# A decoder layer on one core: the last batch taken out of the loop, and the choice of tokens for the experts split between batches 0 to 2 and batch 3

## The chip, the cores and the metric

One core of a Trainium2 chip runs the whole layer in one launch. The metric is the device time in microseconds (us) of that core; less is better. The median of three runs of the kernel before is 4139.88 us (4139.71 to 4147.63).

## The reference, cut to what matters

Four batches of S = 1024 tokens with D = 512 numbers each pass through self-attention (16 heads, relative bias), a layer norm, causal cross-attention against a context, a second layer norm (its result is called x2 below), a mixture of 16 experts, and a last layer norm. The change is about the experts and what stands just before them.

```python
logits = jnp.einsum('bsd,de->bse', x, Wg) + bg
probs = jax.nn.softmax(logits, axis=-2)          # over the 1024 tokens of a batch
pv = jnp.transpose(probs, (0, 2, 1))             # batch, expert, token
vals, idx = jax.lax.top_k(pv, K)                 # K = 128 tokens per batch and expert
tok = x[bidx, idx]
h = relu(tok @ w1[e] + b1[e]); h = relu(h @ w2[e] + b2[e]); h = h @ w3[e] + b3[e]
outputs = zeros.at[bidx, idx].add(h * vals[..., None])
# then layernorm(x + outputs)
```

Each expert picks its 128 tokens out of every batch by itself, so what batches 0 to 2 send to the experts is known as soon as these batches' x2 is. Batch 3 has no part in it.

## The kernel before, in words

There are two blocks of instructions, one after the other, in which each of the five engines (PE, DVE, ACT, POOL, SP) has its own program. Semaphores tie the programs together. The first block ends at line 1377.

**The first block, attention.** Every engine has a loop over the 4 batches. In one batch: eight pairs of heads of self-attention (`attend`; on DVE `add_biases` for a pair's row tiles 2 to 7 and `cross_border` for tiles 0 and 1 of the next pair, where PE weighs the values in three parts, L1088); the output projection with wo (PE L1173, DVE adds at L837); the first norm; the projections for cross-attention; 48 units of cross-attention (`xscore` L1294, `xturn` L1308, `xweigh` L1323, `turn_back` L1331); the second norm (`normalize_rows`, DVE L714 to L726; ACT takes the root at L536). Then x2 is stored twice by SP (L467), as `x2_d` to gather from and as `y_d` to add to, and its rows are turned (PE L988; the even tiles are copied by ACT L541, the odd ones by DVE L734) and multiplied with Wg to logits (PE L1373), which DVE copies (L972) and SP stores (L475). At its end each iteration already opens self-attention of the next batch: PE projects q and k (L1020, partly in the last units of cross-attention), DVE and ACT copy them (L742, L553) and add the bias and take exponentials of four tiles (L756, L530), POOL scales them (L487), DVE turns them (L781). Batch 3 does this too, for a batch of zeros that nobody reads.

**The second block, choosing.** SP loads all logits as 128 rows (64 of batch and expert, each cut into two halves of 512 tokens; L1481). DVE takes the maximum (L1672), ACT the exponentials (L1588), DVE scales. Then DVE picks the 128 largest of each row in 16 rounds of eight (L1682 to L1685, each instruction followed by a wait for its own end), adds the row's base (L1688), PE turns the two lists (L1804) and reverses the upper halves (L1808), and DVE merges the two halves (L1696 to L1701). POOL gathers the tokens of expert 0 (L1547), PE turns them (L1815), ACT and DVE copy them.

**The second block, experts.** A loop over experts 0 to 13 on every engine. PE runs three layers over all four batches at once, each layer 16 products in two passes (L1830, L1845, L1856; 512 columns). DVE applies bias and relu (L1724), and bias and weight of the result (L1735). POOL gathers the next expert's tokens and adds the results to `y_d` (L1569). DVE turns the gathered tokens in blocks of 32 (L1712), and ACT issues 16 DMAs that spread the blocks into `tokT` (L1599). SP loads the three weights of the next expert, each when PE frees its buffer (L1492). Behind the loop experts 14 and 15 run in six steps, for batches (0, 1), (2) and (3) in turn (`STEPS`; PE L1880, L1892, L1901), with the last norm and the output between them. Their weights are loaded at L1496 and L1500, expert 15's tokens are gathered behind the loop, and SP spreads them with 16 DMAs (L1505) into `last_tokT`.

The order on each engine is written out by hand: an engine that waits holds everything behind it in its program, its DMAs too.

```python
            next_tokens(E - 1)                                # POOL, behind the loop
            ...
            sp.wait_ge(tok_turned, B)                         # SP, L1502
            for g in range(GROUPS):
                for m in range(GROUPS):
                    sp.dma_start(last_tokT[...], tok_blocks[...]).then_inc(last_tokT_loaded, 16)
```

## Time and profile before

| what | value |
|---|---|
| median of three runs | 4139.88 us |
| the profiled execution | 4138.08 us |
| its span, first to last instruction | 4136.3 us |
| mean granted TensorE clock | 0.978 |
| PE busy | 3837.9 us (93%) |
| DVE busy | 2483.1 us (60%) |
| ACT busy | 1566.9 us (38%) |
| POOL busy | 904.0 us (22%) |

Times in the rows are microseconds from the first instruction of the profiled execution, so its own 4138.08 us hold 1.8 us outside the span. The four batches fill the time up to about 3361 us, the choice of tokens the time up to 3434 us, the loop over 14 experts that up to 4011 us, and the steps of the last two experts with the last norm the rest.

### The profile page before, as it was taken

Reading aid. Unit: us, or ns where it says so; the run is one execution under the profiler, and the core shown is the slowest. Engines: PE = TensorE matmul, PEld = TensorE weight load, DVE = VectorE, ACT = ScalarE, POOL = GpSimd, SP = SyncE. Lnnn points to the kernel's source line nnn. Section 1 sums busy time; section 2 is a strip of 40 time slices with the busy share of each in tenths; the row PEclk is TensorE's granted clock in tenths of the full one; section 3 lists DMA queues with packets and bytes.
Section 4 is the critical chain, followed back from the end, with each engine's and each line's share of the span. In section 5 each row is a group of like instructions: output and inputs, shape, how many; then the busy total and the mean of one; then the engine's idle time right before and its main releaser. Section 6 shows DMA issues by size and latency. Waiting matters only on the chain. (4 is left out here: it accounts for less than half of the span.)

```text
span 4136.3 us, 91192 instructions
## 1 busy us (share of the span) xinstructions
PE 3837.9 (93%) x36924; PEld 2346.8 (57%) x36924; DVE 2483.1 (60%) x4839; ACT 1566.9 (38%) x3178; POOL 904.0 (22%) x1017
## 2 busy tenths in 40 slices
PE   5999999999999999999999999999999948999996
PEld 2677645656776456567754565677545623444445
DVE  3777535877775368777744587777446872222224
ACT  2444225854442258544422584444135720000002
POOL 2333200223331012233310022333101202222221
PEclk8999999999999999999999999999999979999998
DMA  8333449744333487443335873433358725666676
GB/s 259 105 92 97 126 169 316 269 130 112 96 95 116 188 310 266 127 116 95 95 104 203 305 265 119 116 96 96 103 221 297 265 86 127 157 147 157 148 181 189
DMA packets 323147, 678.60 MB, mean 164 GB/s; under 512 B 28432, under 2 KB 125760, under 8 KB 319504
## 3 DMA queue, kind: packets, MB, share of 16 engines
q1 hardware_dynamic: 275152, 621.65, 46.9%
q0 software_dynamic: 15024, 34.41, 4.5%
q10 hardware_dynamic: 32576, 16.92, 1.9%
q8 instruction: 291, 4.77, 0.5%
q14 instruction: 104, 0.85, 0.1%
HBM read 388.31 MB, written 210.11 MB: 145 GB/s over the span
## 5 line engine op out<-in xcount | busy, mean ns | idle before, releaser
L530 ACT ACTIVATE sc<-sc,nmax 128x1024 f32<-128x1024 f32 x516 | 591.7, 1147 | 777.0 <-DVE nmax L756 776.4
L487 POOL TENSOR_SCALAR sc<-sc,pinv 128x1024 f32<-128x1024 f32 x516 | 576.5, 1118 | 1198.8 <-DVE pinv L764 1185.6
L1088 PE MATMUL psum<-pts,wct 32*64 32x256 f32 x8192 | 460.2, 376 | 9.0 <-PEq L1083 4.6
L1088 PE MATMUL psum<-xall,wct 32*64 32x256 f32 x8192 | 458.9, 376 | 6.1 <-issue 6.0
L1073 PE MATMUL psum<-xt,w_all 128*128 128x256 f32 x1792 | 415.7, 385 | 23.6 <-PEq L1070 23.6
L886 DVE CUSTOM_DVE_ANT_0 sc<-psum,big 128x896 f32<-128x896 f32 (+7 forms) x512 | 364.0, 753 | 102.9 <-PE psum L1294 87.2
L781 DVE STREAM_TRANSPOSE pts<-sc 128x1024 f32<-128x1024 f32 (+3 forms) x342 | 333.6, 976 | 130.6 <-PE psum L1088 87.0
L1073 PEld LDWEIGHTS psum<-xt,w_all 128*128 128x128 f32 x1792 | 332.5, 190 | 128.3 <-issue 67.0
L530 ACT ACTIVATE sc<-sc,xmax 128x896 f32<-128x896 f32 (+7 forms) x512 | 394.8, 773 | 11.7 <-DVE xmax L886 11.6
L756 DVE CUSTOM_DVE_ANT_0 sc<-psum,table_a 128x1024 f32<-128x1024 f32 x258 | 312.1, 1210 | 110.0 <-PE psum L1031 92.5
L1088 PEld LDWEIGHTS psum<-pts,wct 32*64 32x64 f32 x8192 | 310.6, 132 | 99.8 <-issue 54.8
L502 POOL TENSOR_SCALAR_AFFINE_SELECT big<-big 128x256 f32<-128x256 f32 (+1 forms) x192 | 92.6, 482 | 1146.7 <-DMA big<-skew_d 1146.6
L1088 PEld LDWEIGHTS psum<-xall,wct 32*64 32x64 f32 x8192 | 321.3, 131 | 15.0 <-issue 10.6
L781 DVE STREAM_TRANSPOSE xall<-sc 128x1024 f32<-128x1024 f32 (+3 forms) x342 | 326.9, 956 | 2.7 <-DVEq L710 1.2
L1308 PE MATMUL psum<-ident,sc 128*128 128x128 f32 x2304 | 313.5, 281 | 7.1 <-ACT sc L530 6.1
L756 DVE CUSTOM_DVE_ANT_0 sc<-psum,table_b 128x1024 f32<-128x1024 f32 x258 | 314.6, 1219 | 0.5
L1308 PEld LDWEIGHTS psum<-ident,sc 128*128 128x128 f32 x2304 | 258.6, 142 | 77.8 <-DVE pts L896 39.8
L1031 PE MATMUL psum<-xall 64*128 64x512 f32 x1040 | 264.3, 627 | 26.0 <-ACTq L529 10.4
L1060 PEld LDWEIGHTS psum<-w_all,xt 128*128 128x128 f32 x2048 | 236.5, 192 | 76.5 <-issue 76.5
L1031 PE MATMUL psum<-big,xall 64*128 64x512 f32 x1024 | 254.4, 615 | 10.3 <-ACTq L529 8.1
L1617 ACT ACTIVATE hid<-psum,bias 128x128 f32<-128x128 f32 x32 | 11.7, 367 | 647.7 <-PE psum L1880 638.8
L1060 PE MATMUL psum<-w_all,xt 128*128 128x128 f32 x2048 | 254.7, 280 | 0.8 <-PEq L1058 0.6
(194 smaller groups left out, 5362.0 us busy)
## 6 DMA issues: line engine op xcount, KB each, us to landing
wct<-xall SPq DMA_DIRECT2D x576, 128.0 KB, 2.4
big<-skew_d SPq DMA_DIRECT2D x48, 1024.0 KB, 5.4
w_sb<-w_dram SPq DMA_DIRECT2D x45, 1024.0 KB, 5.7
big<-skew_d SPq DMA_DIRECT2D x48, 768.0 KB, 4.4
big<-skew_d SPq DMA_DIRECT2D x32, 896.0 KB, 5.3
big<-skew_d SPq DMA_DIRECT2D x32, 640.0 KB, 7.0
w_all<-wqkv_dram SPq DMA_DIRECT2D x33, 512.0 KB, 3.5
skew_d<-pts SPq DMA_DIRECT2D x8, 2048.0 KB, 6.6
```

Source lines behind the costliest of these rows:

```text
L487: pool.tensor_scalar(sc[k % 4][:, :], sc[k % 4][:, :], pinv[:, k % 4:k % 4 + 1], 1.0, ALU.mult, ALU.mult).then_inc(probs_scaled, 1)
L502: pool.affine_select(out=near, in_=near, compare_op=ALU.is_ge, fill=-BIG, base=0, pattern=[[0, len(heads)], [-1, P]], channel_multiplier=1 ...
L530: act.activation(tile, tile, ACT.Exp, bias=least, scale=-1.0, accum_out=total).then_inc(probs_ready, 1)
L756: dve.tensor_tensor_reduce(sc[k % 4][:, :], SLOT[h], table[h][:, off:off + S], -1.0, BIG, ALU.add, ALU.min, nmax[:, k % 4:k % 4 + 1]).then ...
L781: ins = dve.transpose(probs_t(h, t, first, last), tile[:, first:last, :])
L886: dve.tensor_tensor_reduce(scx[u % 2][:, at], SCORES[:, at], skw[u % 4][:, at], -XSCALE, BIG, ALU.add, ALU.min, xmax[:, k:k + 1]).then_inc ...
L1031: mm = pe.matmul(psum[:, 2 * h + n, :], qf[which][HEAD[h], P * t:P * t + P], kf[which][HEAD[h], HALF * n:HALF * n + HALF], start=True, sto ...
L1060: mm = pe.matmul(SPARE[m // 2][:, P * (m % 2):P * (m % 2) + P], xt[:, c, P * m:P * m + P], w_sb[:, 2, c, :], start=(c == 0), stop=(c == DC ...
L1073: mm = pe.matmul(SPARE[m], w_sb[:, a, c, :], xt[:, c, QG * m:QG * m + QG], start=(c == 0), stop=(c == DC - 1))
L1088: mm = pe.matmul(OSUM[HEAD[h], a, :], v_all[rows, ST * (b % GROUPS) + b // GROUPS, HEAD[h]], ptf[h][rows, QG * b:QG * b + QG], start=(b == ...
L1308: mm = pe.transpose(TURN[m % 3][:, P * (i % 4):P * (i % 4) + P], scx[u % 2][:, at:at + P], ident[:, :])
L1617: act.activation(hid[layer][:, c, cols], BANK[DC * (1 - layer) + c][:, 0:n], ACT.Relu, bias=(bias1, bias2)[layer][:, e:e + 1]).then_inc(st ...
```

## The change

The loops over batches run over batches 0 to 2, and batch 3 is written out behind them (`batch(B - 1, last=True)`).

In batch 3: SP loads the logits of batches 0 to 2 (96 rows) into the upper half of `xr`; DVE runs their selection among the pairs of self-attention, twelve rounds of eight picks at the borders of pairs and four when the output projection begins; PE turns and reverses the lists at row tiles 5 and 6 of the output projection; POOL gathers expert 0's tokens of these batches in the middle of cross-attention, and SP loads w1 and w2 of expert 0 there instead of what the batch of zeros needed. The opening of a fifth batch is gone. The logits of batch 3 are not stored; SP moves them inside SBUF with 8 DMAs.

In the second block: experts 0 to 2 run in three steps over batches 0 to 2 (384 columns), with weights of their own for experts 1 and 2, and then in three steps over batch 3 alone (128 columns). ACT applies bias, relu and weights in these six steps. DVE meanwhile selects for batch 3 (32 rows), and a round of eight picks waits for itself twice instead of three times. PE turns the lists in the step of expert 2. Expert 15's tokens are gathered and spread, and its weights loaded, before the loop. The loop covers experts 3 to 13, and the six steps of experts 14 and 15 stand behind it as before.

```diff
+FIRST_EXPERTS = (0, 1, 2)
+F = len(FIRST_EXPERTS)
+SOONER, LATER = (0, 1, 2), (3,)
-STEPS = [(e, group) for group in FINISH for e in LAST_EXPERTS]
+STEPS = [(e, group) for group in (SOONER, LATER) for e in FIRST_EXPERTS] + \
+        [(e, group) for group in FINISH for e in LAST_EXPERTS]
+BEHIND = 2 * F
...
+            def pick(r):
+                now = held[r][0:n, :]
+                eight = top[0:n, 8 * r:8 * r + 8]
+                done(dve.max(eight, now))
+                ins = dve.max_index(top_at[0:n, 8 * r:8 * r + 8], eight, now)
+                if r < PICKS - 1:
+                    ins = dve.match_replace(held[r + 1][0:n, :], eight, now, -1.0)
+                done(ins)
...
# DVE, batch 3
+                    row_max()
+                    cross_border(scale_rows)
+                    add_biases()
+                    pick(0)
+                    for hp in range(2, PAIRS):
+                        cross_border(lambda: pick(2 * hp - 3))
+                        add_biases()
+                        if hp < PAIRS - 1:
+                            pick(2 * hp - 2)
+                    dve.wait_ge(y_ready, 1)
+                    for r in range(2 * PAIRS - 4, PICKS):
+                        pick(r)
+                    number_rows()
...
# SP, batch 3: the second half of xr once the picks are made; at its end the logits
+                    sp.wait_ge(picked, 1)
+                    sp.dma_start(xr[:, ST // 2:ST, :], x[b, HALF:S, :]...).then_inc(xr_loaded, 16)
...
+                    for i in range(2):
+                        for j in range(2):
+                            for k in range(2):
+                                g = 2 * (i ^ j) + k
+                                sp.dma_start(last_pr[E * i:E * i + E, j, QG * k:QG * k + QG],
+                                             last_lg[DH * g:DH * g + E, :]).then_inc(lg_loaded, 16)
...
# PE, batch 3
+                if last:
+                    first_tokens(pe, 0)
+                    transpose_rows()
...
# POOL, batch 3, middle of cross-attention
+                    if last and u == NU // 2:
+                        pool.wait_ge(picks_done, 1)
+                        pool.wait_ge(xt_free, 1)
+                        for b in SOONER:
+                            pool.indirect_dma_start(tok[:, b, :], None, x2_d[0:S * len(SOONER), :], ...)
...
# SP, second block, ahead of the loop (w3 of expert 0, weights of experts 1 and 2, then expert 15's)
+            sp.wait_ge(early_turned, B)
+            sp.sem_inc(tok_free, 1)
+            sp.wait_ge(tokT_free, 1)
+            sp.sem_inc(tokT_free, -1)
+            spread(tokT, tok_blocks, tokT_loaded)
+            sp.wait_ge(early_turned, 2 * B)
+            sp.sem_inc(tok_free, 1)
+            spread(last_tokT, last_blocks, last_tokT_loaded)
-            with sp.Fori(0, E - 2) as e:
+            with sp.Fori(F, E - 2) as e:
                 for n, w in enumerate((w1, w2, w3)):
                     sp.wait_ge(we_free[n], 1)
...
# POOL, second block
+            gather_sooner(1)
+            for s in range(F):
+                for i in range(2):
+                    scatter(s, i)
+                if s + 2 < F:
+                    gather_sooner(s + 2)
+                scatter(s, 2)
+                if s + 2 == F:
+                    gather_later()                 # waits for picks_done of batch 3
+            pool.wait_ge(first_turned, DC * (F + 1))
+            gather(F)
+            gather_last()                          # waits for tok_free
+            for s in range(F, BEHIND):
+                scatter(s, 0)
...
# ACT, second block
+            for s in range(F):
+                bend(s, 0)
+                bend(s, 1)
+                if s == 0:
+                    row_exps(act, 1, last_pr[0:2 * LATER_ROWS, :, :])
+                    act.wait_ge(bias3_scaled, 1)
+                take_y(s, 0)
+                take_y(s, 1)
+                copy_first_tokens(act, s + 1, tokT if s < F - 1 else later_tokT)
+                take_y(s, 2)
...
# PE, second block, in take_step(s): first layer
+                    mm.then_inc(step_hid_full, 1)
+                    if s == F - 1 and o == 0:
+                        turn_picks(pe, 1, row_no[:, :], (BANK[0][:, 0:P], BANK[0][:, P:2 * P]))
+                    if s == F - 1 and o == 1:
+                        flip_picks(pe, 1, LATER_ROWS, flip[:, :], lists, BANK[1][:, 0:2 * LATER_ROWS])
...
+            for s in range(BEHIND):
+                take_step(s)
+            pe.wait_ge(step_y_taken, TAKEN[BEHIND])
             pe.sem_inc(y_taken, B)
-            with pe.Fori(0, E - 2) as e:
+            with pe.Fori(F, E - 2):
```

New names used below: `first_tokens` turns the gathered tokens of three batches on PE (12 transposes), `bend` is bias and relu on ACT, `take_y` bias and weight on ACT, `spread` the 16 DMAs from turned blocks to the layout that PE reads.

## Rows read from the trace of the kernel before

**Rows 1.** The page, busy tenths of 40 equal slices (103.4 us each).

```profile
PE   5999999999999999999999999999999948999996
PEclk8999999999999999999999999999999979999998
```

**Rows 2.** Windows: stretch, length, busy us (x instructions) by engine, clock, DMA share, GB/s.

```profile
3390.00:3400.00 10.00, 0.00 (x0) 0.00 (x0) 8.39 (x19) 0.00 (x0) 0.00 (x0) 0.50 0.00 1
```

**Rows 3.** Timeline, end of batch 3: start us, us, engine, line, what.

```profile
3340.43 3.74 DVE L726 TENSOR_SCALAR xr<-xr,mv,rstd 128x512 f32<-128x512 f32 x8 [0.15 <-DVEq L710]
...
3357.20 0.69 DVE L734 COPY wct<-psum 128x512 f32<-128x512 f32 x1
...
3358.75 1.92 PE L1373 MATMUL psum<-wct,wg_sb 128*16 128x256 f32 x32 [1.83 <-PEq L995]
...
3361.80 1.86 SPq L475 DMA_DIRECT2D logit_d<-big  x4
...
3364.03 1.20 DVE L781 STREAM_TRANSPOSE xall<-sc 128x1024 f32<-128x1024 f32 x1
3365.49 2.46 SPq L1481 DMA_DIRECT2D pr<-logit_d  x4
```

**Rows 4.** Timeline, choosing tokens.

```profile
3370.25 1.22 DVE L1672 TENSOR_REDUCE rmax<-pr 128x1 f32<-128x1024 f32 x1 [5.03 <-DMA pr<-logit_d]
...
3374.62 0.69 DVE L1682 MAX8 top<-pr 128x8 f32<-128x512 f32 x1
...
3377.27 0.70 DVE L1682 MAX8 top<-left 128x8 f32<-128x512 f32 x1
...
3416.51 0.48 PE L1804 MATMUL psum<-ident,row_no 128*128 128x128 f32 x1 [55.84 <-DVE row_no L1688]
...
3429.49 3.30 PE L1815 MATMUL psum<-ident,tok 128*128 128x128 f32 x16 [10.86 <-DMA tok<-x_d,idx_g]
...
3433.90 13.97 PE L1830 MATMUL psum<-tokT,w_sb 128*128 128x512 f32 x32 [1.10 <-PEq L1828]
```

**Rows 5.** Groups by line and form, 3434 to 4010 us.

```profile
L1830 PE MATMUL psum<-tokT,w_sb 128*128 128x512 f32 x448 | 194.6, 592 | 1.1 <-PEq L1828 1.1
```

**Rows 6.** Timeline, from the end of the loop on.

```profile
4010.77 7.07 PE L1880 MATMUL psum<-tokT,w_sb 128*128 128x256 f32 x32
...
4023.13 0.95 POOL L1547 DMA_INDIRECT tok<-x_d,idx_g  x1 [0.30 <-issue]
...
4027.69 10.56 SPq L1505 DMA_DIRECT2D last_tokT<-tok_blocks  x16
...
4040.64 10.14 PE L1880 MATMUL psum<-last_tokT,last_w 128*128 128x256 f32 x32 [7.13 <-DMA last_tokT<-tok_blocks]
...
4064.39 3.73 PE L1880 MATMUL psum<-tokT,w_sb 128*128 128x128 f32 x32
...
4075.02 3.73 PE L1880 MATMUL psum<-last_tokT,last_w 128*128 128x128 f32 x32
```

**Rows 7.** Timeline of DVE at a border of two pairs of heads, batch 3.

```profile
2733.60 1.25 DVE L781 STREAM_TRANSPOSE xall<-sc 128x1024 f32<-128x1024 f32 x1
2735.46 1.23 DVE L756 CUSTOM_DVE_ANT_0 sc<-psum,table_a 128x1024 f32<-128x1024 f32 x1 [0.62 <-PE psum L1031]
...
2742.71 0.71 DVE L781 STREAM_TRANSPOSE pts<-sc 128x512 f32<-128x512 f32 x1 [3.30 <-PE psum L1088]
...
2751.83 0.45 DVE L781 STREAM_TRANSPOSE pts<-sc 128x256 f32<-128x256 f32 x1 [1.00 <-ACTq L581]
```

**Rows 8.** Timeline of DVE in the output projection, batch 3.

```profile
2961.88 0.69 DVE L837 TENSOR_TENSOR xr<-psum,xr 128x512 f32<-128x512 f32 x1 [20.01 <-PE psum L1173]
...
2983.34 0.69 DVE L837 TENSOR_TENSOR xr<-psum,xr 128x512 f32<-128x512 f32 x1 [5.24 <-PE psum L1173]
```

**Rows 9.** DMA issues in 3440 to 3900 us: what, count, KB each, median us to landing.

```profile
w_sb<-w_dram SPq DMA_DIRECT2D x34, 1024.0 KB, 5.7
...
tok<-x_d,idx_g POOLq DMA_INDIRECT x44, 3.7
```

595 lines of the change are left out of this document (382 added, 213 removed).

## The prediction, made before the changed kernel ran

> **What bounds the kernel now.** I read the slices of the page first. PE is the engine that is busy nearly always, at full clock, and there is one dip besides the end [rows 1]. A window in that dip shows PE idle and the clock at 0.50, while DVE alone works [rows 2]. So elsewhere the time is PE's work, and here it is a chain. The timeline gives the chain in two pieces. First, the end of batch 3: DVE normalises x2 until 3344.2, PE turns the rows in between other work until DVE's last copy ends at 3357.9, the logits are multiplied from 3358.75 to 3360.7, SP stores them at 3361.8, and SP's next load comes at 3365.49, right behind DVE's last turn for the batch of zeros, which ends at 3365.2 [rows 3]: the blocks are closed by all engines together. Second, the choice: it starts at 3370.25, a round of eight picks takes 3377.27 - 3374.62 = 2.65 us and there are 16, the lists are turned at 3416.5, the first tokens reach PE at 3429.5, and the first expert's product starts at 3433.9 [rows 4]. From the logits' end (3360.7) to there PE does some 4 us of work in 73 us.
>
> The experts themselves are PE from end to end: 448 products of the first layer have 1.1 us of idle before them in all [rows 5]. Fourteen passes of the loop take 4010.77 - 3433.90 = 576.9 us, 41.2 us each [rows 4, 6].
>
> The last thing to see stands behind the loop. Expert 14's step on batches 0 and 1 starts at 4010.77, expert 15's at 4040.64, after a wait of 7.13 us for `last_tokT`, and expert 15's ends at 4064.39 [rows 6]. At 256 columns a layer of 16 products takes half of 41.2 / 3, and the third layer of two batches the same, so a step is 20.6 us. The first took 29.9 and the second 23.75 (its first layer ran 10.14 us where the step before needed 7.07: PE had stood still and restarted slowly). Together 12.4 us are lost there to the late gather and its 16 DMAs.
>
> **The change part by part.** I follow the time at which the loop over the remaining experts can start, against 3433.9 + 3 x 41.2 = 3557.5, when the kernel before has done experts 0 to 2.
>
> *End of batch 3.* With no fifth batch, PE turns the rows at once. DVE's odd copies start at 3343.9 (0.4 us is won, because PE's q products no longer stand in front of the last turns of cross-attention), and there are four of them (0.69 us each), with PE's four transposes and two handoffs between; I take 1.8 us for each period, so 3350.2. Logits 1.92, DVE's copy and the handoffs 0.9: 3353.2. Then SP issues 8 small DMAs before it can close its block. Four took 1.86 us at L475 and four 2.46 at L1481 [rows 3], mean 0.54, so 8 cost 4.3. With handoffs and slower transposes (PE is idle for some 5 us before them) the second block starts at 3359; from 3356 to 3362.
>
> *Three steps over batches 0 to 2.* 384 columns are three quarters of 41.2 us: 30.9 each, 92.7 us. PE has stood 5 us, so it starts at half the clock, as expert 15's step did, which lost 3.07 us [rows 6]; I take 3.0. Turning the next tokens: 16 transposes took 3.30 us at the low clock [rows 4], so 12 at the full one take 1.3; with the switch 1.5, three times: 4.5. Turning and reversing batch 3's lists in the third step: 1.5 (PE 0.5 + 0.7 and handoffs). The weights hide: a load lands in 5.7 us [rows 9], and before the second step 4 are wanted, 22.8 us even one after the other, against more than 30.
>
> Does batch 3's selection come in time? ACT's exponentials stand behind two layers' `bend`, so they start about 3.0 + 20.6 + 0.7 us into the block. Exponentials with their table 3, DVE's scaling 1.2, 16 rounds at 2.65 less 0.2 for the wait dropped = 39.2, row numbers 0.4: picks at 68.1 us into the block. PE wants them after 3.0 + 61.8 + 3.0 + 2.6 = 70.4. A margin of 2 us, so nothing is waited for; if a round takes 2.65 still, 1 us is.
>
> So the three steps end at 3359 + 3.0 + 92.7 + 4.5 + 1.5 = 3460.7.
>
> *Three steps over batch 3.* A step of one batch took 4075.02 - 4064.39 = 10.63 us [rows 6], although a quarter of 41.2 is 10.3. Three: 31.9, so PE is ready for the loop at 3492.6. But is the loop? Its first w1 is issued by SP behind two `spread`s, and those wait for gathers. POOL adds the last result of the third step (2.7 us with ACT's part), then copies indices and gathers 4 tiles for expert 3: the last gather is issued some 5 us later, 8.3 us behind the step's end. From a last gather's issue to SP's first spread DMA it took 4027.69 - 4023.13 = 4.6 us, and 16 such DMAs hold SP's queue for 10.56 us [rows 6]. Expert 15's gathers start only when the blocks are turned; they land and are turned just as the first spread ends (3.8 for the issues, 3.7 to landing [rows 9], 2.5 for DVE = 10.0). Then the second spread, 10.56, then the w1 load, 5.7 [rows 9]. Sum: 8.3 + 4.6 + 10.6 + 10.6 + 5.7 = 39.8 us behind the three steps, against PE's 31.9. **PE waits some 8 us for w1**, as long as the wait in rows 6, so I charge the slow restart again, 3.0. The loop is as good as started at 3460.7 + 39.8 + 3.0 = 3503.5. That is 54.0 us sooner than 3557.5.
>
> The Trainium skill has a rule against this step, in "DMA: Bandwidth & Descriptors", section "Issuing engines are not separate DMA queues": issuing from several engines saves only sequencer time, usually small beside the transfer. By it the 32 DMAs in front of w1 would cost little; the row has 10.56 us of SP's queue for 1 MB, and I go by the row.
>
> *Behind the loop.* Gather, turn, spread and weights of expert 15 are gone from there: 12.4 us are won, and the rest of the tail follows PE.
>
> *Costs in batch 3.* Twelve rounds of 2.45 us on DVE in self-attention. At a border, DVE idles 0.6 us before `open_pair(0)` and 3.3 us before the turn that waits for PE [rows 7]; the round placed there fits. The other round, between pairs, pushes the opening by 1.9 us, and the two together push the turns by about 1.1; the next idle microsecond (before 2751.83) takes it up. Nearest rows say 0; bounds 0 and 12 x 2.45 = 29.4. I take 1.0. Four more rounds when the projection begins: 10 us from 2961.9, while PE begins its fifth tile one period (5.24 + 0.69 + 0.93) before 2983.34, at 2976.5, and needs only the first sum for it; DVE idles 5.2 us before each later tile [rows 8], so nothing but PE's three list instructions: 1.5. POOL's three gathers in cross-attention hold its queue for 4 us; they cost 0 if its masks are made that far ahead, and 4 if they are wanted at once. POOL is busy for 22% of the time, so I take 0.
>
> **The sum:** 54.0 + 12.4 - 1.0 - 1.5 = 63.9. The profiled execution had 4138.08, 1.8 less than the median 4139.88, so 4074.2 against it and **4076.0** as a median.
>
> **The rivals.** (a) *The forecast*: w1 late behind the spreads. 4076, from 4068 to 4084 by the bounds of the block's start (3 each way), of the restarts (0 to 6) and of the pairs. Chance 0.55.
>
> (b) *w1 is not waited for*: the issue queue moves faster than in rows 6, because nothing else loads then, or PE's small steps take longer than 10.6 with their handoffs to ACT. PE is the bound throughout; 10.9 us more are won: 4065, to 4061 with an early start of the block. This is what the skill's rule above would give. For it: the buffer of w1 is free some 25 us before the load is issued. Against: 16 DMAs held ACT's and SP's queues alike. Chance 0.2.
>
> (c) *The selection costs on both sides*: the rounds are on the path in half of the borders (15 us), or the picks of batch 3 come a few us after PE wants them (my margin is 2). 4084 to 4100, typically 4090. For it: 0.6 us is all the idle time before a pair's opening. Chance 0.2.
>
> (d) *Slower*: PE runs dry at the borders, and each time its clock falls. The place is the border of two pairs, 12 rounds. The gain without them is 64.9 us; a round costs what it delays, 2.45, if both waits of rows 7 move with it 4.9, and with a restart at half clock 3.07 more: 8.0, 96 us in all, so 4171. It decides from (64.9 + 8.3) / 12 = 6.1 us a round. [...] Chance 0.03.
>
> (e) *The change doesn't do what it says*: PE's steps wait for batch 3's picks anyway, through one of the queues (POOL waits for `picks_done` with adds behind it, ACT for the exponentials). Then only the phantom batch's end, some 6 us, and the 12.4 remain: about 4122. Against it: in no queue does a step of batches 0 to 2 stand behind such a wait before the third. Chance 0.02.
>
> **How the numbers follow.** The forecast is (a)'s, 4076. The range takes (a), (b) and most of (c): 4061 to 4096. The measurement tells some 0.2% from no change, 8.3 us. Faster 0.95 ((a), (b), (c) nearly whole, (e)); slower 0.03, from (d); the same 0.02.
>
> **What would show it.** In the profile after: the first product of the experts at about 3359, at clock 0.5; three layers of 16 products of 384 columns, 10.3 us each; the lists turned in the third step with a PE idle below 1 us before it; a wait of PE for w1 ahead of the loop, 8 us, with SP's `last_tokT` spread ending just before the load; no wait for `last_tokT` behind the loop, so 41.2 us for the two steps there; pairs of self-attention in batch 3 as long as in batch 2. Wrong would be: a w1 wait of none (b), or of far more; longer pairs; a wait of PE for the picks.

## The result and the profile after

| | before | changed |
|---|---|---|
| time, median of the runs shown together | 4143.76 us (4139.71 to 4147.98) | 4077.09 us (4071.49 to 4081.91) |
| ratio | | 0.9839, 95% interval 0.9820 to 0.9857 |
| profiled execution: its time, span | 4138.08, 4136.3 us | 4071.49, 4069.7 us |
| TensorE's mean granted clock | 0.978 | 0.984 |

The changed kernel is 1.6% faster. The forecast was 4076.0 us. Between the two profiled executions lie 66.6 us, where the sum said 63.9.

The page of the changed kernel, busy tenths of 40 slices (101.7 us each):

```profile
PE   5999999989999999899999999999999989999997
...
PEclk8999999999999999999999999999999999999998
```

The dip to 4 of [rows 1] is an 8 now, and the clock's 7 beside it is a 9. Two short pauses are what is left of it. Both stand in the timeline of PE, of SP and of DVE at the end of batch 3 and after it (start us, us, engine, line, what, idle time ahead):

```profile
3333.33 0.33 PE L1573 MATMUL psum<-ident,wct 128*128 128x128 f32 x1 [0.38 <-ACT wct L862]
...
3350.58 3.26 PE L1620 MATMUL psum<-wct,wg_sb 128*16 128x256 f32 x32 [1.63 <-issue]
3353.88 0.48 DVE L1193 TENSOR_SCALAR w_and_tables<-psum,bg_sb 128x256 f32<-128x256 f32 x1 [4.20 <-PE psum L1620]
3354.61 5.20 SPq L642 DMA_DIRECT2D w_and_tables<-w_and_tables  x8
3360.65 12.54 PE L2112 MATMUL psum<-xt,w_and_tables 128*128 128x384 f32 x32 [6.82 <-PEq L2088]
...
3394.96 10.48 PE L2112 MATMUL psum<-xt,fin 128*128 128x384 f32 x32
...
3425.94 0.27 DVE L370 TENSOR_SCALAR row_no<-top_at,base_sb 32x128 f32<-32x128 uint32 x1
3427.21 2.74 PE L2112 MATMUL psum<-xt,fin 128*128 128x384 f32 x8
3429.79 0.27 PE L325 MATMUL psum<-ident,row_no 128*128 128x128 f32 x1
...
3459.91 3.73 PE L2112 MATMUL psum<-later_tokT,w_and_tables 128*128 128x128 f32 x32
```

`L2112` is the first layer of a step. The first step starts at 3360.65, right behind SP's 8 DMAs (to 3359.81), and its first layer takes 12.54 us where the second step's takes 10.48: the clock was low. The picks are numbered by 3426.2 (`L370`), and the lists are turned at 3429.79 with no wait, 3.6 us later. The three steps over batches 0 to 2 end at 3459.91. The windows show the clock (stretch, length, busy us by engine, clock, DMA share, GB/s):

```profile
3359.00:3363.00 4.00, 2.35 (x4) 1.47 (x5) 1.70 (x4) 0.00 (x0) 1.56 (x2) 0.50 0.37 80
3363.00:3365.00 2.00, 2.00 (x5) 0.96 (x5) 0.00 (x0) 0.00 (x0) 1.29 (x2) 0.59 1.00 363
3365.00:3395.00 30.00, 30.00 (x95) 16.66 (x94) 6.47 (x18) 10.51 (x19) 4.54 (x4) 1.00 1.03 359
...
3492.00:3498.00 6.00, 0.47 (x2) 0.00 (x0) 0.00 (x0) 0.78 (x1) 1.56 (x1) 0.98 0.68 117
3498.00:3504.00 6.00, 2.28 (x3) 1.17 (x4) 0.00 (x0) 0.00 (x0) 3.12 (x5) 0.50 1.05 390
```

The second pause is the one that the prediction charged, ahead of the loop (SP, ACT, DVE and PE in one timeline):

```profile
3469.09 2.03 DVE L1991 STREAM_TRANSPOSE tok_blocks<-xt 128x512 f32<-128x512 f32 x3 [34.38 <-DMA xt<-x_d,idx_g]
...
3472.22 10.70 SPq L1728 DMA_DIRECT2D xt<-tok_blocks  x16
...
3481.29 2.49 DVE L1991 STREAM_TRANSPOSE last_blocks<-xt 128x512 f32<-128x512 f32 x4 [9.23 <-DMA xt<-x_d,rows]
3483.42 0.78 ACT L1902 ACTIVATE oute<-psum,scaled_bias,vals 128x512 f32<-128x512 f32 x1 [5.12 <-DMA y_d<-oute,rows]
3483.87 10.82 SPq L1728 DMA_DIRECT2D last_tokT<-last_blocks  x16
...
3492.51 0.78 ACT L1902 ACTIVATE oute<-psum,scaled_bias,vals 128x512 f32<-128x512 f32 x1 [3.07 <-PE psum L2146]
...
3495.10 1.00 SPq L1743 DMA_DIRECT2D w_and_tables<-w_dram  x2
...
3501.72 15.40 PE L2170 MATMUL psum<-xt,w_and_tables 128*128 128x512 f32 x32 [9.24 <-PEq L2168]
```

PE had its last result at 3492.5. SP's two spreads stand in front of w1, which goes out at 3495.10, and PE starts the loop at 3501.72, after 9.24 us. Its first 32 products take 15.40 us, where the same 32 in the loop of before took 13.97 [rows 4]. Behind the loop nothing is waited for:

```profile
3956.42 7.07 PE L2112 MATMUL psum<-xt,w_and_tables 128*128 128x256 f32 x32
...
3977.10 7.07 PE L2112 MATMUL psum<-last_tokT,last_w 128*128 128x256 f32 x32
...
3997.78 3.73 PE L2112 MATMUL psum<-xt,w_and_tables 128*128 128x128 f32 x32
```

The two steps take 3997.78 - 3956.42 = 41.36 us; they took 4064.39 - 4010.77 = 53.62 [rows 6].

In batch 3's self-attention, the border that [rows 7] show has become (timeline of DVE):

```profile
2733.66 1.25 DVE L977 STREAM_TRANSPOSE xall<-sc 128x1024 f32<-128x1024 f32 x1
2734.83 0.65 DVE L362 MAX8 top<-xr 96x8 f32<-96x512 f32 x1
...
2737.33 1.23 DVE L952 CUSTOM_DVE_ANT_0 sc<-psum,w_and_tables 128x1024 f32<-128x1024 f32 x1 [0.30 <-DVEq L945]
...
2741.19 0.67 DVE L362 MAX8 top<-xr 96x8 f32<-96x512 f32 x1
```

The opening of the pair comes at 2737.33 instead of 2735.46. One pair earlier the first round starts at 2682.96, so that a pair is 2734.83 - 2682.96 = 51.87 us long, as before the change (51.86 us between the same rows of two pairs): the late opening is made up within the pair. In the output projection four rounds stand ahead of DVE's sums, and PE's later tiles are reached some 0.7 us late (2984.08 for the sum of 2983.34 in [rows 8]), 1.1 us at its end. In these two profiles cross-attention gave even that back: the last turn of batch 3 stands at 3333.33, and it stood at 3333.42. That is one profile of each kernel. From the end of self-attention (DVE's last turn there starts at 2940.50) to that last turn this profile of the changed kernel has 392.8 us, as the one of before has, and all ten profiles of the runs below have 395.4 to 401.5, though none of them edits anything in this stretch. So what the change costs in batch 3 is known to within some 9 us only.

### The profile page after: what moved, and what is told of

Its sections match the earlier page's. It is cut to its first block and busy times, and to the rows that moved or that the text cites. A ratio compares the mean times of both kernels' runs of the same rounds, so it can differ in the third digit from the quotient of the medians.

```text
span 4069.7 us, 91371 instructions
## 1 busy us (share of the span) xinstructions
PE 3828.7 (94%) x37104; PEld 2365.1 (58%) x37104; DVE 2471.1 (61%) x4870; ACT 1598.8 (39%) x3247; POOL 897.9 (22%) x1005
## 5 line engine op out<-in xcount | busy, mean ns | idle before, releaser
L952 DVE CUSTOM_DVE_ANT_0 sc<-psum,w_and_tables 128x1024 f32<-128x1024 f32 x512 | 603.6, 1213 | 97.9 <-PE psum L1267 81.7
L1310 PE MATMUL psum<-xt,w_and_tables 128*128 128x256 f32 x1792 | 415.7, 385 | 23.0 <-PEq L1307 23.0
L1310 PEld LDWEIGHTS psum<-xt,w_and_tables 128*128 128x128 f32 x1792 | 332.5, 190 | 127.7 <-issue 66.3
L1325 PEld LDWEIGHTS psum<-xall,wct 32*64 32x64 f32 x8192 | 324.4, 131 | 17.1 <-issue 12.3
L1550 PEld LDWEIGHTS psum<-ident,sc 128*128 128x128 f32 x2304 | 257.2, 142 | 77.3 <-DVE pts L1122 39.8
L1297 PEld LDWEIGHTS psum<-w_and_tables,xt 128*128 128x128 f32 x2048 | 236.3, 192 | 75.4 <-issue 75.4
L1892 ACT ACTIVATE hid<-psum,bias 128x128 f32<-128x128 f32 (+1 forms) x80 | 34.3, 431 | 594.1 <-PE psum L2112 554.7
L1297 PE MATMUL psum<-w_and_tables,xt 128*128 128x128 f32 x2048 | 254.5, 280 | 0.6 <-PEq L1295 0.5
L1536 PE MATMUL psum<-xall 32*128 32x512 f32 (+3 forms) x1024 | 204.1, 589 | 46.7 <-DVE xmax L1112 34.2
```

Of the source, the lines that this page charges most:

```text
L952: dve.tensor_tensor_reduce(sc[k % 4][:, :], SLOT[h], table[h][:, off:off + S], -1.0, BIG, ALU.add, ALU.min, nmax[:, k % 4:k % 4 + 1]).then ...
L1297: mm = pe.matmul(SPARE[m // 2][:, P * (m % 2):P * (m % 2) + P], xt[:, c, P * m:P * m + P], w_sb[:, 2, c, :], start=(c == 0), stop=(c == DC ...
L1310: mm = pe.matmul(SPARE[m], w_sb[:, a, c, :], xt[:, c, QG * m:QG * m + QG], start=(c == 0), stop=(c == DC - 1))
L1325: mm = pe.matmul(OSUM[HEAD[h], a, :], v_all[rows, ST * (b % GROUPS) + b // GROUPS, HEAD[h]], ptf[h][rows, QG * b:QG * b + QG], start=(b == ...
L1536: mm = pe.matmul(SCORES[:, at:at + m], q, k, start=True, stop=True)
L1550: mm = pe.transpose(TURN[m % 3][:, P * (i % 4):P * (i % 4) + P], scx[u % 2][:, at:at + P], ident[:, :])
```

## The experiments

All are edits of the changed kernel. Their medians carry an interval of about 0.15% (6 us), as wide as most of the effects, and one source of that is visible: the last turn of batch 3, which no edit below touches except the two on the picks, lay between 3333.3 and 3343.4 us in the profiles. So I read stretches of PE's timeline: **border**, from that last turn to the first step; **steps**, from there to the first step over batch 3; **to loop**, from there to the loop's first product; **behind**, the two steps behind the loop.

| run | median us | ratio [95%] | border | steps | to loop | behind |
|---|---|---|---|---|---|---|
| changed kernel | 4077.09 | 0.9839 [0.9820, 0.9857] | 27.32 | 99.26 | 41.81 | 41.36 |
| weights first | 4070.46 | 0.9836 [0.9823, 0.9850] | 28.03 | 99.70 | 38.97 | 41.36 |
| spread behind | 4065.68 | 0.9821 [0.9806, 0.9836] | 28.18 | 99.22 | 35.24 | 41.36 |
| open sooner | 4067.00 | 0.9824 [0.9809, 0.9839] | 23.29 | 97.27 | 42.40 | 41.35 |
| double picks | 4098.46 | 0.9901 [0.9886, 0.9917] | 28.91 | 98.85 | 42.72 | 41.36 |
| three rounds | 4086.28 | 0.9865 [0.9849, 0.9882] | 28.09 | 99.70 | 43.30 | 41.36 |
| late picks | 4082.23 | 0.9856 [0.9841, 0.9871] | 28.05 | 107.93 | 43.21 | 41.36 |
| late picks, early exponentials | 4081.62 | 0.9850 [0.9835, 0.9865] | 27.87 | 99.54 | 42.77 | 41.36 |
| expert 15 late again | 4079.97 | 0.9853 [0.9838, 0.9868] | 28.20 | 99.18 | 33.57 | 53.47 |
| picks first | 4123.98 | 0.9958 [0.9941, 0.9975] | 71.53 | 99.65 | 41.65 | 41.36 |
| together | 4059.11 | 0.9799 [0.9786, 0.9812] | 23.19 | 97.28 | 32.01 | 41.36 |

A stretch is read from one profile of each run, and it varies where nothing was edited. Seven kernels have the same code from the first step over batch 3 to the loop (changed kernel, open sooner, double picks, three rounds, late picks, its companion, picks first): they need 41.65 to 43.30 us for it, and their first 32 products of the loop take 15.40 to 16.76 us. Both together the changed kernel's profile is the lowest, by up to 2.7 us, so a gain at this place that is read against it may be up to 2.7 us too small.

**The overlap itself: picks first.** My theory of the gain was that three steps run where PE stood idle.

```diff
+            row_exps(act, 1, last_pr[0:2 * LATER_ROWS, :, :])
             for s in range(F):
                 bend(s, 0)
                 bend(s, 1)
                 if s == 0:
-                    row_exps(act, 1, last_pr[0:2 * LATER_ROWS, :, :])
                     act.wait_ge(bias3_scaled, 1)
...
+            pe.wait_ge(picked, 2)
             for s in range(BEHIND):
                 take_step(s)
```

> Edit of the changed kernel: TensorE waits for batch 3's picks before the first expert step, and ACT does batch 3's exponentials ahead of the first bends, so that nothing is overlapped with the selection. Theory (the gain of the change is that three steps over batches 0 to 2 run in the time in which PE waited for the picks): the picks come 39.2 us behind the exponentials (3386.99 to 3426.2), these now at about 3365.4, so PE starts the first step at about 3404.6 instead of 3360.65, 44 us later, and 0 to 2 us more for the clock; all that follows keeps its length (steps 97 to 99 us, then 41.8 us to the loop, the two steps behind the loop 41.4 us). Time 4077 + 45 = about 4122, ratio to before 0.994 to 0.997. Rival: the gain is mostly elsewhere (batch 3 written out without a fourth batch's loads, the tail), and this costs under 25 us.

The border is 71.53 us, 44.2 more, and nothing else moved. The row of PE's timeline:

```profile
3414.90 12.93 PE L2112 MATMUL psum<-xt,w_and_tables 128*128 128x384 f32 x32 [49.46 <-PEq L2088]
```

So 44 of the 66.6 us hang on the overlap. By the medians 16 us are left against the kernel before, with an interval of some 7 us either way. By the profiles 12.3 are left behind the loop, and from batch 3's last turn to the end of the loop 9.5 (667.8 us against 677.4), in which the end of batch 3, the cheaper rounds and the tokens gathered ahead of the block are not told apart.

**The wait for w1: weights first, spread behind.**

```diff
+            for n, w in enumerate((w1, w2)):
+                sp.wait_ge(we_free[n], 1)
+                sp.sem_inc(we_free[n], -1)
+                sp.dma_start(w_e[n], w[F].rearrange("(c p) n -> p c n", p=P)).then_inc(we_loaded[n], 16)
             sp.wait_ge(early_turned, B)
             sp.sem_inc(tok_free, 1)
...
+            sp.wait_ge(we_free[2], 1)
+            sp.sem_inc(we_free[2], -1)
+            sp.dma_start(w_e[2], w3[F].rearrange("(c p) n -> p c n", p=P)).then_inc(we_loaded[2], 16)
-            with sp.Fori(F, E - 2) as e:
+            with sp.Fori(F + 1, E - 2) as e:
```

> Edit of the changed kernel: w1 and w2 of expert 3 are issued by SP ahead of the two spreads (16 DMAs each), w3 behind them. In the changed kernel SP's queue is held 10.70 and 10.82 us by the spreads, w1 goes out at 3495.10 and PE waits for it until 3501.72, 9.24 us, and then runs its first 32 matmuls of the loop in 15.40 us instead of about 13.7. Theory A (w1 stands behind the spreads in SP's queue, and this alone holds PE): PE waits only until ACT has taken the last result, about 3493.4, and the clock stays at 1.00: the loop starts 8 us sooner and loses 1.7 us less, in all 10 us, time about 4067, profiled about 4061.5. Theory B (the other transfers of this stretch, or the last gathers, would hold PE in its place): the loop starts at most 3 us sooner. Rival C (the first iteration inside the loop runs dry on the tokens of expert 4 when it starts sooner): a new wait of several us behind the first iteration, total gain under 5 us.

The wait is gone, 1.51 us are left for the copy of the last result, and the clock was high when the loop began (13.97 us for 32 products). But only 2.8 + 1.4 us were won, since other waits had taken its place (DVE, POOL, ACT and PE):

```profile
3477.54 0.71 DVE L1998 STREAM_TRANSPOSE tok_blocks<-xt 128x512 f32<-128x512 f32 x1 [0.34 <-DMA xt<-x_d,idx_g]
...
3484.10 1.62 POOL L1832 DMA_INDIRECT y_d<-oute,rows  x1 [0.30 <-issue]
...
3489.61 0.78 ACT L1909 ACTIVATE oute<-psum,scaled_bias,vals 128x512 f32<-128x512 f32 x1 [8.44 <-DMA y_d<-oute,rows]
...
3490.44 1.74 PE L2119 MATMUL psum<-later_tokT,fin 128*128 128x128 f32 x8 [3.56 <-ACT oute L1909]
3491.97 4.83 PE L2139 MATMUL psum<-hid,fin 128*128 128x128 f32 x32
...
3501.74 13.97 PE L2177 MATMUL psum<-xt,w_and_tables 128*128 128x512 f32 x32 [1.51 <-PEq L2175]
```

The 2 MB of w1 and w2 now move from 3467 on, together with the gathers of expert 3. Those were issued at the same place (3.9 us behind the step's start in both), and the last of the four was turned 14.8 us behind it instead of 11.4. POOL waits for that turn before it gathers expert 15, and behind those gathers in POOL's order stands the scatter of batch 3's first result, which ACT's next result must wait for (8.44 us), and PE waits for ACT (3.56 us). The clock fell in that pause too: it was 0.50 from 3492 to 3494, and the 32 products behind it took 4.83 us instead of 3.79. Theory A was right about what held PE, and wrong that this alone did. It is theory B of the expectation that took most of the gain, through the gathers, at another place than w1.

```diff
             sp.wait_ge(early_turned, 2 * B)
             sp.sem_inc(tok_free, 1)
-            spread(last_tokT, last_blocks, last_tokT_loaded)
...
                 sp.dma_start(w_e[n], w[E - 2].rearrange("(c p) n -> p c n", p=P)).then_inc(we_loaded[n], 16)
+            spread(last_tokT, last_blocks, last_tokT_loaded)
```

> Edit of the changed kernel: only the 16 DMAs that spread the tokens of expert 15 are moved, from ahead of the loop's weight loads to behind the last of them; the gathers and turns of expert 15 stay where they are. By theory A, that the place in SP's queue is what costs, w1 of expert 3 goes out at about 3484 instead of 3495.10 (SP then waits only for the turned tokens, 3483.9), lands about 3490, and PE starts the loop at about 3493.4: 10 us gained, as with the weights first, and the two steps behind the loop keep their 41.4 us, since 16 DMAs issued in the last iteration are through long before they are needed. If bandwidth or descriptors in flight were the limit (theory B), w1 would not land before about 3498 and the gain is under 4 us. If the tail needs the early spread, the two steps behind the loop grow from 41.4 us towards the 53.6 us of before.

```profile
3490.49 0.96 SPq L1742 DMA_DIRECT2D w_and_tables<-w_dram  x2
...
3501.26 13.97 PE L2170 MATMUL psum<-xt,w_and_tables 128*128 128x512 f32 x32 [1.60 <-PEq L2168]
```

The load of w1 goes out 24.5 us behind the first step over batch 3 (3490.49 - 3466.02) instead of 35.2, and PE waits 1.60 us. From 41.81 to 35.24 us, and 1.4 more by the clock: 8.0 of the 10 expected, with the tail's 41.36 kept. The same 16 DMAs cost 7 us or more at one place of SP's queue and nothing at another. A stall of PE of 1.27 us, "ACT hid", that the changed kernel's profile does not have accounts for most of the rest; a stall of 1.2 to 1.4 us stands there in five other runs too (double picks, three rounds, late picks, its companion, picks first). What causes it stays open. Against the profiles that have it the gain is 8.1 to 10.7 us, stretch and first products together.

**The block's border: open sooner.**

```diff
                 if last:
-                    for i in range(2):
-                        for j in range(2):
-                            for k in range(2):
-                                g = 2 * (i ^ j) + k
-                                sp.dma_start(last_pr[E * i:E * i + E, j, QG * k:QG * k + QG],
-                                             last_lg[DH * g:DH * g + E, :]).then_inc(lg_loaded, 16)
                     return
...
         @block2.sync
         def _(sp):
+            for i in range(2):
...
```

> Edit of the changed kernel: the 8 small DMAs that rearrange batch 3's logits (5.20 us of SP's queue, 3354.61 to 3359.81) are issued as the first of the second block instead of the last of the first, so that the block closes without them. Theory A: PE starts the first step at about 3355.5 instead of 3360.65, and with a shorter pause loses less to the low clock; but the picks of batch 3 come at the same absolute time (3426.2, lists turned about 3429.8), which is now wanted 5 us sooner than before, while the margin read from the trace was 3.6 us: PE waits about 1.5 us at the lists, in the third step. Net gain 3 to 5 us, the three steps end 3455 to 3457 instead of 3459.91. Rival: the picks have no such margin to give (a margin under 1 us) and the whole 5 us are lost again at the lists; rival 2: the block's border costs the same whatever SP does, and the first step starts at 3360 still.

```profile
3355.25 3.46 PE L1614 MATMUL psum<-wct,wg_sb 128*16 128x256 f32 x32 [1.58 <-issue]
...
3359.95 10.56 PE L2112 MATMUL psum<-xt,w_and_tables 128*128 128x384 f32 x32 [1.24 <-PEq L2088]
...
3384.31 0.15 DVE L354 TENSOR_TENSOR rinv<-rsum 32x1 f32<-32x1 f32 x1 [15.51 <-ACT w_and_tables L338]
...
3427.11 0.27 PE L325 MATMUL psum<-ident,row_no 128*128 128x128 f32 x1
```

The border is 4.0 us shorter and the steps 2.0, 6.0 in all (the wait ahead of the loop is as before, 42.40 us, and lies in the range given above): the first layer ran at the full clock behind a pause of 1.24 us, with the clock still low in the logits' products (3.46 us against 1.92 in [rows 3]). My fear for the picks was wrong. The lists are not waited for, since DVE still waits 15.51 us for ACT's exponentials: what starts the picks is their place in ACT's order, behind the second `bend`, and that moved with PE.

**The margin of batch 3's picks: late picks, with and without early exponentials.**

```diff
             for r in range(PICKS):
                 pick(r)
+                if r < 4:
+                    pick(r)
```

> Edit of the changed kernel: the first 4 of the 16 rounds that pick batch 3's tokens in the second block are done twice (idempotent), 4 x 2.38 = 9.5 us more on DVE between the exponentials (done 3386.99) and the lists. In the changed kernel the picks were ready at 3426.2 and the lists' transposes wanted them at 3429.79, 3.6 us later, with no wait. Theory A (the margin is 3.6 us): PE waits 9.5 - 3.6 = 5.9 us ahead of the lists' transposes in the third step, and 0 to 3 us more go to the clock that falls in the pause; the time from the first matmul of the second block to the first step over batch 3 grows from 99.26 to 105 to 108 us, and the whole by as much. Rival: the picks are needed later than I read, only by the gathers for batch 3 behind the third step, so that nothing or under 2 us is lost.

```profile
3437.86 0.48 PE L325 MATMUL psum<-ident,row_no 128*128 128x128 f32 x1 [5.82 <-DVE row_no L370]
```

PE waits 5.82 us for 9.5 more of picking, so the margin was 3.7 us. The steps took 8.7 us more in all. Beside the wait that is 0.5 in the first layer of the first step (13.00 us against 12.54; the unedited profiles run from 12.1 to 13.0 there) and 2.4 behind the wait, at the low clock (the first transpose of the lists took 0.48 us instead of 0.27).

```diff
                 bend(s, 0)
+                if s == 0:
+                    row_exps(act, 1, last_pr[0:2 * LATER_ROWS, :, :])
                 bend(s, 1)
                 if s == 0:
-                    row_exps(act, 1, last_pr[0:2 * LATER_ROWS, :, :])
                     act.wait_ge(bias3_scaled, 1)
```

> Edit: the same 4 repeated rounds, and besides ACT does the exponentials of batch 3's logits between the first and the second layer of the first step instead of behind both. In the changed kernel DVE waited 24.44 us (3362.5 to 3386.99) for those exponentials, because they stand behind both layers in ACT's order; the run with the block opened sooner had no wait at the lists either, though its logits came as late as before, which says that ACT's order and not the logits' arrival sets when the picks start. Theory A: the picks start about 3372 to 3375 (12 to 15 us sooner), more than the 9.5 us added, so PE does not wait at the lists and the stretch is 99.3 us again (up to 2 us more where the exponentials and their table load, 2.8 us, delay the bends of the second layer). Rival: something other than ACT's order starts the picks, and PE waits as in the run with late picks alone.

```profile
3384.20 0.15 DVE L354 TENSOR_TENSOR rinv<-rsum 32x1 f32<-32x1 f32 x1 [14.40 <-ACT w_and_tables L338]
...
3437.32 0.27 PE L325 MATMUL psum<-ident,row_no 128*128 128x128 f32 x1
```

No wait, and the steps are 99.54 us again. The exponentials are done 16.3 us behind the first product (3384.20 - 3367.89) instead of 26.3 (3386.99 - 3360.65): 10.0 us sooner, less than the 12 I had written. The medians of the two runs do not tell them apart; the stretch does.

**Picking at the borders of the pairs: double picks, three rounds.**

```diff
                     pick(0)
+                    pick(0)
                     for hp in range(2, PAIRS):
-                        cross_border(lambda: pick(2 * hp - 3))
+                        cross_border(lambda: (pick(2 * hp - 3), pick(2 * hp - 3)))
                         add_biases()
                         if hp < PAIRS - 1:
                             pick(2 * hp - 2)
+                            pick(2 * hp - 2)
```

> Edit of the changed kernel: each of the 12 rounds of picking at the borders of the pairs in batch 3's self-attention is done twice (the second is an idempotent repeat), 12 rounds of 2.4 us more on DVE, 29 us in all. In the changed kernel a pair at its border is 51.86 us long with and without the picks, and the turn behind the pick had 0.22 us of waiting left of 3.30. Theory A (rounds are free only up to the slack; what goes over it stands on the path): between 1.5 and 4.4 us more per pair, 6 to 7 pairs, 10 to 29 us in all. Rival B (DVE has slack to recover within a pair, about 100 us of DVE in 500 are idle): 0 to 3 us in all, pairs stay at 51.9 us. Rival C (the late turns let PE run dry and its clock falls): over 35 us.

First the first instruction of all rounds of batches 0 to 2, in the changed kernel and in this run (shortest, median and longest in ns, first and last start in us), then two borders of this run:

```profile
L362 DVE MAX8 top<-xr x16: 647/671/691, 2630.8 to 2969.7; 96x8 f32<-96x512 f32 x16
L362 DVE MAX8 top<-xr x28: 647/691/693, 2626.1 to 2989.0; 96x8 f32<-96x512 f32 x28
...
2793.69 0.65 DVE L362 MAX8 top<-xr 96x8 f32<-96x512 f32 x1
...
2850.66 0.65 DVE L362 MAX8 top<-xr 96x8 f32<-96x512 f32 x1
```

This pair is 56.97 us long, 5.1 more than 51.86, and it is the longest of five: they run from 55.37 to 56.97, mean 56.06, so 4.2 more for two added rounds of 2.37. The whole stretch from the first round to the last one is 24.0 us longer (362.9 against 338.9) for 12 rounds, 2.0 each; the ratios say 26 (0.9901 - 0.9839 of 4143). Most of it is on the path. The third round alone, with only the place behind `add_biases` doubled:

```diff
                         if hp < PAIRS - 1:
                             pick(2 * hp - 2)
+                            pick(2 * hp - 2)
```

> Edit of the changed kernel: at the borders of the pairs of batch 3's self-attention only the round behind the add of the biases is done twice, 6 rounds of 2.37 us more on DVE. With two rounds a border a pair was 51.86 us as without any; with four (both doubled) it was 56.97 us, 5.1 us more for 4.75 us of DVE time. Theory A (two rounds have used up the cover: 0.22, 0.44 and 0.20 us of waiting left behind them): a pair with three rounds is 53.4 to 54.4 us, 9 to 15 us more in all. Rival B (the border has cover for a third round in the second place, the damage came from the first place alone): pairs stay under 52.3 us and the whole costs under 3 us.

```profile
2685.12 0.65 DVE L362 MAX8 top<-xr 96x8 f32<-96x512 f32 x1
...
2738.49 0.65 DVE L362 MAX8 top<-xr 96x8 f32<-96x512 f32 x1
```

53.37 us here; five pairs run from 53.01 to 53.63, mean 53.28, so 1.4 us more for 2.37 of work. The 11 us in all by the ratios have some 10 us of interval either way; the stretch from the first round to the first one of the output projection is better: 339.8 us, where it is 330.6 to 331.8 in nine profiles with two rounds a border and 355.7 with four. So six third rounds cost 8 us, 1.3 each, and six fourth ones 16 us, 2.7 each, about their own length (2.4). The 5.1 us for 4.75 that the expectation gives for four rounds were those of the longest pair. Two rounds a border cost nothing that can be seen, a third is hidden by almost half, a fourth not at all. The third was only tried in the second place and the fourth only in the first, so number and place are not told apart.

**The tail: expert 15 late again.** The gathers of expert 15 are one more pass of the loop's `next_tokens`, DVE turns them inside the first step behind the loop, and SP spreads them last, as in the kernel before:

```diff
-            sp.wait_ge(early_turned, 2 * B)
-            sp.sem_inc(tok_free, 1)
-            spread(last_tokT, last_blocks, last_tokT_loaded)
...
-            gather_last()
...
+            next_tokens(E - 1)
             for s in range(BEHIND, len(STEPS)):
```

> Edit of the changed kernel: expert 15's tokens are gathered, turned and spread behind the loop again, as in the kernel before (one more turn of POOL's loop body, DVE's turn inside the first step behind the loop, SP's 16 DMAs behind it); the rest of the change stays. Theory A: the two steps over batches 0 and 1 behind the loop take 53.6 us again instead of 41.4 (12.2 us more, PE waits for the spread ahead of expert 15); in exchange only one spread stands ahead of w1 of expert 3, which goes out about 3483 and lands before the last step's result is taken (3493.3), so that the wait of 9.24 us and the 1.5 us of slow clock at the loop's start go. Net 1 to 3 us slower than the changed kernel. Rival: w1 is late all the same (the wait stays over 5 us), then 7 us or more slower; rival 2: the tail's wait was not the spread of expert 15, then the steps stay at 41.4 us and the kernel is 10 us faster.

```profile
3496.79 13.97 PE L2172 MATMUL psum<-xt,w_and_tables 128*128 128x512 f32 x32 [1.51 <-PEq L2170]
...
3979.95 9.99 PE L2114 MATMUL psum<-last_tokT,last_w 128*128 128x256 f32 x32 [7.07 <-DMA last_tokT<-tok_blocks]
```

Both terms in one run: the tail costs 12.1 us again (53.47 against 41.36), and the loop starts 8.2 us sooner and keeps 1.4 of clock. Net 2.4 us slower by the stretches, and against the highest of the other profiles of the unedited stretch the difference is gone; the ratios say 6 us with an interval of some 10. The early gather of expert 15 was worth 12.1 us behind the loop and paid 9.7 of them back in front of it, by the other profiles up to 12.3.

**Together.** Five moves: w1 and w2 of expert 3 between the two spreads, behind expert 3's gathers; expert 15's spread behind the last load; batch 3's logits moved in the second block; PE no longer waits for the last result except ahead of the fourth bank; POOL scatters batch 3's first result before it gathers expert 15.

```diff
             spread(tokT, tok_blocks, tokT_loaded)
+            for n, w in enumerate((w1, w2)):
+                sp.wait_ge(we_free[n], 1)
+                sp.sem_inc(we_free[n], -1)
+                sp.dma_start(w_e[n], w[F].rearrange("(c p) n -> p c n", p=P)).then_inc(we_loaded[n], 16)
             sp.wait_ge(early_turned, 2 * B)
...
+            scatter(F, 0)
             gather_last()
-            for s in range(F, BEHIND):
+            for s in range(F + 1, BEHIND):
...
-            pe.wait_ge(step_y_taken, TAKEN[BEHIND])
-            pe.sem_inc(y_taken, B)
+            pe.sem_inc(y_taken, B - 1)
...
+            act.wait_ge(step_y_taken, TAKEN[BEHIND])
+            act.sem_inc(y_taken, 1)
```

> Edit of the changed kernel, five moves together: SP issues w1 and w2 of expert 3 between the two spreads (behind the gathers of expert 3, which loads put out sooner had made 5 us late in the run with the weights first) and w3 behind; the spread of expert 15's tokens goes behind the last weight load; the 8 small DMAs of batch 3's logits open the second block; PE no longer waits for the last result to be taken except ahead of the layer's fourth bank; POOL scatters the first result of batch 3 ahead of the gathers of expert 15. Theory A: block opened sooner 6.0 us (measured alone: 4.0 at the border, 2.0 by the clock in the first step); the wait ahead of the loop 9.2 + 1.4 us of clock + 0.7 of small stalls + about 0.9 for the result's copy = 11 to 12 us: together 17 to 18 us sooner than the changed kernel, the loop's first matmul 31.9 to 32.5 us behind the first step over batch 3 (41.8 in the changed kernel). Time about 4059, ratio to before 0.979 to 0.981. Rival: one of the moves takes away the cover of another (the transfers of w1 and w2 against the gathers of expert 15, the picks against the sooner block) and the sum is under 12 us.

```profile
3363.02 10.56 PE L2122 MATMUL psum<-xt,w_and_tables 128*128 128x384 f32 x32 [1.24 <-PEq L2098]
...
3460.30 3.73 PE L2122 MATMUL psum<-later_tokT,w_and_tables 128*128 128x128 f32 x32
...
3492.31 13.90 PE L2179 MATMUL psum<-xt,w_and_tables 128*128 128x512 f32 x32
```

The loop's first product follows the last small step with no idle time. From batch 3's last turn to the end of the loop the time is 605.7 us (3945.51 - 3339.83) against 623.1 in the changed kernel (3956.42 - 3333.33): 17.4 us, and 16.6 by the ratios. Of these 4.1 lie in the border, 2.0 in the steps, 9.8 ahead of the loop and 1.5 in its first products. The two moves on PE's wait and on POOL's scatter have no run of their own, so what each is worth stays open. At 4059.11 us, ratio 0.9799 [0.9786, 0.9812], it beats both kernels; its interval and the changed kernel's (0.9820 to 0.9857) do not meet.

## Why the prediction was right

The forecast, case (a), came true with its mechanism. Point by point:

- **The second block's start**: 3359 forecast, 3360.65 measured. The 8 DMAs of SP took 5.20 us, 0.65 each, where I took the 0.54 of `L475` and `L1481` [rows 3]; the logits' products took 3.26 us instead of 1.92, at the low clock, where I had left "slower transposes" to a round number; each copy period was 1.50 us (3344.48 to 3348.99 for three) instead of 1.8.
- **The restart in the first step**: 3.0 forecast from [rows 6], 2.1 measured (12.54 - 10.48). Together with the start the errors nearly cancelled: the three steps ended at 3459.91, forecast 3460.7.
- **The selection in time**: yes. The forecast margin was 2 us; it was 3.6 in the trace, and 3.7 by the run with late picks. A round took 2.38 us on 32 rows, where I took 2.45.
- **The wait for w1**: 8 us forecast, 9.24 measured (in the changed kernel's trace, by PE's own idle time). The load went out at 3495.10, 35.2 us behind the steps' end, where my chain said 34.1. The restart behind it was charged at 3.0; it took 1.4 here (15.40 - 13.97), and 1.7 to 2.8 in the six other profiles with this wait, so 3.0 was less wrong than this trace makes it look. "As good as started" at 3503.5 was 3503.2 (3956.42 less 11 passes of 41.2).
- **Luck in the sum**: the loop's start came within 0.3 us because terms that were each off by 1 to 2.5 us cancelled: the block's start 1.7 later, the three steps 2.4 shorter (99.26 against 101.7, of which 0.9 is the restart), the stretch to the loop 2.0 longer (41.81 against 39.8), its restart 1.6 cheaper.
- **Behind the loop**: 12.4 forecast, 12.3 measured, and 12.1 with the gather put back.
- **The costs in batch 3**: 1.0 for the pairs and 1.5 for the projection. Measured 0 and 1.1, and that was made up before the batch ended. This is where the 2.7 us of difference between sum and trace come from, together with 0.3 of the start of the loop. But the 0 rests on the two profiles whose last turns lie 0.1 us apart; with the 2.6 to 8.6 us that the other ten profiles have on this one, a cost of 2.5, or of 5, would not be seen. That includes POOL's three gathers, which were taken at 0 and which no run isolates.

The Trainium skill's rule of "DMA: Bandwidth & Descriptors", section "Issuing engines are not separate DMA queues", was rival (b)'s ground: sequencer time usually small beside the transfer. For one DMA the trace agrees in part: each took 0.67 us of SP's queue and landed after 2.1 us. For the whole it does not: 16 DMAs of 64 KB held SP's queue for 10.70 and 10.82 us, and moving 16 of them to another place won 8.0 us. The same section also says that DMAs started by different engines run on the same 16 DMA engines and interleave. That agrees with the trace of the run with the weights first, where 2 MB started by SP delayed the last of POOL's gathers by 3.3 us.

Rival (c) fell in both of its halves for the change as made, but it was close: a third round at a border is paid for by more than half, and the picks of batch 3 had 3.7 us to spare. My argument for the pairs had been "the next idle microsecond takes it up", and it did. Rival (d) needed 6.1 us a round; the twelve rounds beyond the first two a border cost 2.0 each, and PE's clock held between 0.97 and 1.00 in those windows of 50 us. A short pause can lower the clock too: the 3.56 us in the run with the weights first did, and a round is 2.4. Rival (e) is what the run with the picks first does: 4124 us, forecast for it 4122.

What I had not seen is that the pause at the block's border could be shortened by the same kind of edit, and that the exponentials' place in ACT's order and not the logits' arrival sets when the picks start. Neither changed the sum.

## What to carry to other kernels

When idle time is filled with work of another stage, look for the first thing behind it that was prefetched under that idle time: here the first weights of the loop stood behind 32 small DMAs in one issuing queue, and the second 16 of them, the price of another part of the same change, made nearly all of the wait (9.24 us with them there, 1.60 and 1.51 us without). Order an issuing queue by when each item is wanted, not by when its data is ready, and check that what goes out sooner doesn't land on the gathers that the chain needs. Slack inside a software pipeline has an edge: two rounds were free, the third cost 1.3 of its 2.4 us, the fourth 2.7, so measure one unit more than is used. And read a stretch from more than one profile: here the same code took 41.65 to 43.30 us.

## What the runs showed of the hardware

- In the run with the block opened sooner and in the one with all moves, the granted clock was 0.50 some 4 to 7 us ahead of the first step, and yet the first layer behind a pause of 1.24 us took 10.56 us, nearly its time at the full 2.4 GHz (10.48). Behind pauses of 6.6 to 8.0 us it took 12.1 to 13.0; in the changed kernel the clock was 0.50 (1.2 GHz) for the first 2.4 us of it and 0.59 in the next two. In the run with the weights first a pause of 3.56 us was enough: the clock was 0.50 behind it, and 32 products of 128 columns took 4.83 us instead of 3.79.
- What a restart costs varies from run to run: behind pauses of 7.9 to 9.6 us the loop's first 32 products (512 columns) took 15.40 to 16.76 us, where 13.90 is their time without a pause.
- A DMA issue on SP took 0.65 us for the 16 KB pieces (5.20 / 8) and 0.67 to 0.69 us for those of 64 KB (10.70 / 16 and 11.00 / 16), so the size of a piece hardly set it. The two loads of 1 MB took 1.00 us together.
- Two loads of 1 MB each, issued from 0.5 us behind the first of four gathers of 128 rows on, moved the arrival of the last gather by 3.3 us and that of the first by 0.8.
